# Output projection of the attention block as three half-precision products in place of one 32-bit product

## The reference, cut to what matters

```
q, k, v = x @ wq.T, x @ wk.T, x @ wv.T          # 16 heads of 64; rotary embedding on q and k
probs = softmax(causal(q @ k.T * scale))
out = probs @ v                                 # (4, 1024, 1024)
out = einsum('btd,od->bto', out, wo)            # output projection, (4, 1024, 128)
x = x + layernorm(out); then the feed-forward part
```

## Time and profile before

| what | value |
|---|---|
| time, median of 3 runs | 1192.29 us (1190.64 to 1192.48) |
| the profiled execution's own time | 1189.41 us |
| its span, first to last instruction | 1187.5 us |
| busy share PE, PEld | 93%, 67% |
| busy share DVE, ACT, POOL | 81%, 81%, 80% |
| granted TensorE clock, mean share of full speed | 0.978 |
| slots 0 to 15 of the attention loop | 62.4 to 941 us |
| feed-forward part | 947 to 1187.5 us |

### The profile page before, as it was taken

One profiled execution on the slowest core, in us unless ns is written; L12 is line 12 of the kernel. 1 busy time (PEld: TensorE's weight loads), 2 busy tenths in 40 slices (PEclk: granted clock), 3 DMA queues, 4 the chain that ended last, 5 costly groups with the idle time before them and its releaser, 6 DMA issues. The chain is left out here.

```text
span 1187.5 us, 36496 instructions
## 1 busy us (share of the span) xinstructions
PE 1110.2 (93%) x14311; PEld 800.0 (67%) x14311; DVE 959.2 (81%) x2195; ACT 956.4 (81%) x2205; POOL 951.1 (80%) x1064
## 2 busy tenths in 40 slices
PE   4689999999999999999999999999998788999996
PEld 1256777777777777777777777777776555666663
DVE  7789787978879797979788797979895359767977
ACT  7767989889797979798897979798887767756574
POOL 3569899999999999999999999999784567434663
PEclk9689999999999999999999999999998999999999
DMA  6761525252533425152515345252611000000011
GB/s 194 167 151 38 144 49 132 73 126 57 143 82 99 106 75 145 39 142 73 134 48 143 79 103 121 61 145 54 163 32 39 15 23 2 1 1 1 2 37 36
DMA packets 50475, 97.24 MB, mean 82 GB/s; under 512 B 8512, under 2 KB 25152, under 8 KB 46272
## 3 DMA queue, kind: packets, MB, share of 16 engines
q1 hardware_dynamic: 50304, 94.92, 31.6%
HBM read 58.47 MB, written 34.60 MB: 78 GB/s over the span
## 5 line engine op out<-in xcount | busy, mean ns | idle before, releaser
L916 POOL TENSOR_TENSOR Plo<-P,Phi 128x512 f16<-128x512 f32 (+3 forms) x634 | 531.6, 866 | 68.1 <-ACT P L566 66.4
L563 ACT ACTIVATE Phi<-psS 128x512 f16<-128x512 f32 (+3 forms) x768 | 394.6, 514 | 125.3 <-PE psS L413 74.1
L566 ACT ACTIVATE P<-psS 128x512 f32<-128x512 f32 (+3 forms) x634 | 313.8, 496 | 0.0
L435 PE MATMUL psO<-V,Plo 128*128 128x65 f16 x2304 | 289.2, 194 | 0.0
L431 PE MATMUL psO<-V,Phi 128*128 128x65 f16 x2304 | 288.6, 193 | 0.6 <-POOL Plo L916 0.6
L433 PE MATMUL psO<-V,Phi 128*128 128x64 f16 x2304 | 287.5, 192 | 0.0
L402 PE MATMUL psS<-Q,K 128*128 128x512 f16 (+3 forms) x768 | 252.8, 329 | 17.6 <-DVE Plo L742 13.0
L431 PEld LDWEIGHTS psO<-V,Phi 128*128 128x128 f16 x2304 | 216.1, 98 | 42.5 <-POOL Plo L916 1.4
L791 DVE TENSOR_REDUCE pmax<-psX 128x1 f32<-128x512 f32 x384 | 242.1, 681 | 0.2
L433 PEld LDWEIGHTS psO<-V,Phi 128*128 128x128 f16 x2304 | 214.9, 97 | 31.2 <-issue 1.1
L435 PEld LDWEIGHTS psO<-V,Plo 128*128 128x128 f16 x2304 | 214.4, 97 | 0.0
(11 more groups left out here) (215 smaller groups left out, 2500.7 us busy)
## 6 DMA issues: line engine op xcount, KB each, us to landing
k_way<-HL SPq DMA_DIRECT2D x64, 256.0 KB, 3.9
K<-k_way SPq DMA_DIRECT2D x32, 512.0 KB, 8.4
q_way<-HL SPq DMA_DIRECT2D x60, 256.0 KB, 3.7
Q<-q_way SPq DMA_DIRECT2D x15, 1024.0 KB, 11.8
K<-k_way SPq DMA_DIRECT2D x32, 256.0 KB, 4.3
Q<-q_way SPq DMA_DIRECT2D x30, 256.0 KB, 5.3
out<-y SPq DMA_DIRECT2D x8, 256.0 KB, 2.2
y<-in_x SPq DMA_DIRECT2D x3, 512.0 KB, 10.4
```

The costliest lines, as they stand in the source:

```text
L435: mm = nc.tensor.matmul(O, M.Plo[:, U % NP_, k * P:(k + 1) * P], V[:, HD:2 * HD + 1], start=False, stop=j == t, skip_group_check=True)
L563: nc.scalar.activation(M.Phi[:, U % NP_, 0:w], X, ACT.Exp, scale=SCALE)
L566: nc.scalar.activation(full, X, ACT.Exp, scale=SCALE).then_inc(S.exp_done, 1)
L916: nc.gpsimd.tensor_tensor(M.Plo[:, U % NP_, 0:w], M.P32[:, U % NP_, 0:w], M.Phi[:, U % NP_, 0:w], ALU.subtract).then_inc(S.lo_pool, 1)
```

## The change

The product is made of 16-bit halves. The transposed output is split by ScalarE (upper half, the same copy as before with a 16-bit output) and by VectorE (lower half: the bank minus the upper half), as is done for V. VectorE now gives the bank back, and `wo` waits for that. The weights are split once: their 32-bit form comes by the same DMA into the second half of `M.OT`, which is free then; ScalarE copies the upper halves at slot 0, step 20, and GpSimd forms the lower ones at step 26. For each chunk TensorE adds three products: upper by upper, upper weights by lower outputs, and lower weights by upper outputs (the product of the two lower halves is left out).

```diff
+WO_HALVES = ((0, 20), (0, 26))
 TR1_STEPS, WO_STEPS, TR0_STEPS = (10, 16), (17, 18), (33, 46)
...
+    ot32 = M.OT[:].rearrange("p w a n -> p (w a n)").bitcast(F32)
+    wo32 = ot32[:, TT * D:2 * TT * D].rearrange("p (k d) -> p k d", d=D)
...
                     if s == 1 and half == 0:
-                        pe.wait_ge(S.wo_in, 16)
+                        pe.wait_ge(S.wo_lo, 1)
                     taken(pe, (s - 1, "tr", 0, half))
                     taken(pe, (s, "tr", 1, half))
                     for k in range(4):
                         for c in range(CH):
                             t = 4 * half + k
-                            mm = nc.tensor.matmul(X[:, k * P:(k + 1) * P], M.OT[:, c, t * P:(t + 1) * P],
-                                                  M.wo[:, CH * og + c, :], start=c == 0, stop=c == CH - 1)
+                            for q, (wi, xi) in enumerate([(0, 0), (0, 1), (1, 0)]):
+                                mm = nc.tensor.matmul(X[:, k * P:(k + 1) * P], M.OT[:, xi, c, t * P:(t + 1) * P],
+                                                      M.wo[:, wi, CH * og + c, :], start=c == 0 and q == 0,
+                                                      stop=c == CH - 1 and q == 2)
...
-                    nc.scalar.copy(M.OT[:, a[0], a[1] * BANK:(a[1] + 1) * BANK], X).then_inc(free(item), 1)
+                    nc.scalar.copy(M.OT[:, 0, a[0], a[1] * BANK:(a[1] + 1) * BANK], X).then_inc(S.turn_hi, 1)
...
+                if (s, u) == WO_HALVES[0]:
+                    act.wait_ge(S.wo_in, 16)
+                    nc.scalar.copy(M.wo[:, 0], wo32).then_inc(S.wo_hi, 1)
...
+                elif kind == "tr":
+                    dve.wait_ge(S.turn_hi, turn[item] + 1)
+                    if turn[item] == 0:
+                        dve.wait_ge(S.wo_lo, 1)
+                    cols = slice(a[1] * BANK, (a[1] + 1) * BANK)
+                    nc.vector.tensor_tensor(M.OT[:, 1, a[0], cols], X, M.OT[:, 0, a[0], cols],
+                                            ALU.subtract).then_inc(free(item), 1)
...
+                if (s, u) == WO_HALVES[1]:
+                    pool.wait_ge(S.wo_hi, 1)
+                    nc.gpsimd.tensor_tensor(M.wo[:, 1], wo32, M.wo[:, 0], ALU.subtract).then_inc(S.wo_lo, 1)
...
-            sp.dma_start(M.wo[:], I["wo"]).then_inc(S.wo_in, 16)
+            sp.dma_start(wo32, I["wo"]).then_inc(S.wo_in, 16)
...
-        M.wo = sb(stack, "wo", [P, HEADS * HD // P, D], F32)
+        M.wo = sb(stack, "wo", [P, 2, HEADS * HD // P, D], F16)
...
-        M.OT = sb(stack, "OT", [P, CH, T], F32)
+        M.OT = sb(stack, "OT", [P, 2, CH, T], F16)
```

More of the change, by code:

```diff
@@ L313, in attention_block @@
     weights = (M.wkq[:, 0], M.wkq[:, 1], M.wv)
+    ot32 = M.OT[:].rearrange("p w a n -> p (w a n)").bitcast(F32)
+    wo32 = ot32[:, TT * D:2 * TT * D].rearrange("p (k d) -> p k d", d=D)
+    turn = {}
+    for key in steps:
+        for item in at.get(key, []):
+            if item[1] == "tr":
+                turn[item] = len(turn)
     w32 = M.P32[:].rearrange("p a n -> p (a n)").rearrange("p (k n) -> p k n", k=3)
@@ L627, in junk @@
             def junk(n):
-                to = M.On if n < 3 * TT else M.OT
                 k = (n - TT) % (2 * TT)
-                return to[:].rearrange("p a n -> p (a n)")[:, k * D:(k + 1) * D]
+                if n < 3 * TT:
+                    return M.On[:].rearrange("p a n -> p (a n)")[:, k * D:(k + 1) * D]
+                return ot32[:, k * D:(k + 1) * D]
             def x_sums(b):
@@ L1961, in build @@
         S.wo_in = sem("wo_in")
+        S.wo_hi = sem("wo_hi")
+        S.wo_lo = sem("wo_lo")
+        S.turn_hi = sem("turn_hi")
         S.w_lo_pool = sem("w_lo_pool")
```

## The result

| kernel | median, us | runs | against the kernel before |
|---|---|---|---|
| before | 1191.11 | 5 | 1 |
| changed | 1199.42 (1198.03 to 1201.86) | 5 | 1.0076, 95% interval 1.0057 to 1.0094 |

The change makes the kernel slower by 0.8%. The profiled execution of the changed kernel took 1201.86 us, the highest of the five, and that of before 1189.41 us, so their difference (12.5 us) is larger than that of the medians (8.3 us).

The account below looks back on a forecast made before the run. It took a chain through GpSimd, ScalarE, VectorE and TensorE as the bound, over GpSimd at the projection. 14 x 0.71 = +9.9, weights +1.0, end -0.5 make +10.4 us; forecast 1201 us, range 1184 to 1213.

Parts of the forecast that it names:

- the saving: Projection on TensorE: 1.04 us a slot spared, 16.6 us in all at most; taken as bringing 0.
- the subtractions at steps 10 and 16: VectorE's added work on chunk 1's transposes: each taken at 0; bounds at step 10 were 0 and 0.60 us.
- the term for step 33: VectorE waits 0.95 us for ScalarE's copy, subtracts ahead of out_scale, delays TensorE: 0.7 us a slot, bounds 0 and 1.55.
- The price of an item: Each projection item on TensorE takes 1.34 us as half-precision products, in place of 1.87 and 1.86 us.
- The new wait: Step 17: the first projection item waits for step 16's subtraction and starts 0.48 us later, so its gain is gone.
- The closed chain: Around a slot: GpSimd up to step 27, ScalarE to step 36, VectorE for one operation, TensorE and ScalarE for the rest.
- GpSimd's unbroken stretch: GpSimd runs 461.31 to 494.69 without a wait; the second item's 0.52 us lie beside it and don't shorten it.
- Step 46 at 0: VectorE's subtraction there is covered by VectorE's own free time: 0, bounds 0 and 0.6 us.
- rival 3: VectorE becomes the bound in steps 8 to 40: 1.7 us a slot lost, 1216 us; chance 0.13.
- The last projection: After the last slot: two items of 1.34 us and a subtraction end it at 945.18, 0.5 us gained.
- The weights' split: Slot 0: one ScalarE copy and one GpSimd operation, taken at 1.0 us, bounds 0 and 2.1.
- The first, TensorE holds the slot: Rival: each slot gets 1.04 us shorter, 1175.7 us in full, 1184 for half; chance 0.29.

Follow-up runs that it names:

- Products only: Changed kernel without VectorE's subtractions, upper half standing in for the lower, ScalarE giving the bank back: 1172.58 us, 0.9853 of the kernel before.
- one step later: Changed kernel with VectorE alone taking the subtraction of step 33 one step later, behind out_scale: 1196.02 us, 1.0053 of the kernel before.
- no lower at 33: Changed kernel without the subtraction at step 33, upper half standing in for the lower: 1192.59 us, 1.0023 of the kernel before.
- subtraction only: Kernel before, 32-bit projection kept, plus VectorE's 64 subtractions into a scratch tile that nothing reads: 1208.75 us, 1.016 of the kernel before.
- lower at 46 alone: Changed kernel with only the subtraction at step 46 kept, upper half standing in elsewhere: 1176.13 us, 0.9877 of the kernel before.

## Why the prediction was right, and where its steps failed

**Direction and size were right**: 1201 forecast, 1199.4 measured; 0.71 us a slot forecast, 0.73 measured in a slot without a DMA wait and 0.97 as the mean. But this is luck in part. Three terms of a slot, each taken at 0, were not 0: the saving, -1.04 us, and the subtractions at steps 10 and 16, +0.60 each. Together they make +0.16, about what the term for step 33 was too high.

**The price of an item** was right: 1.34 us, 1.05 us spared per slot.

**"The new wait" of the first item was wrong.** I read the waits ahead of `wo` as if item 0 needed the subtraction of step 16. `taken(pe, (s, "tr", 1, half))` asks for that of its own half, step 10, which is long done. There is no wait, and both items give back their 0.52 us.

**The closed chain, and "lie beside GpSimd's unbroken stretch", were wrong.** I took a stretch of 33 us without a wait as the sign of the engine that sets the pace, and closed the chain with ScalarE's wait for the last Plo of it. Products only showed neither to hold: the wait behind GpSimd's stretch shrank by 0.84 us, and ScalarE's wait at step 28 was for TensorE's scores, which had come within 0.01 us of that Plo. The sign I gave too little weight was TensorE's own: its idle times sum to 0.40 us in slot 7 of the kernel before. The saving was taken at 0; in products only it is 1.06 us in a slot without a DMA wait, and in the changed kernel 1.02 - 0.64 = 0.38 is left of it. The subtraction at step 16 takes the rest.

**Step 10 and step 16, each taken at 0,** cost 0.60 us each: the upper bound that I gave for step 10. The cover named for them, GpSimd's stretch, wasn't one.

**Step 33 was right in its mechanism and somewhat too high.** The wait was 0.90 us (0.95 forecast), and TensorE's delay in steps 33 to 37 0.81 us (0.71). I had the chain without slack until it closes, but 0.26 us come back in steps 37 to 41, so that 0.54 of the 0.71 is left. The wait for V was swallowed on VectorE and not on TensorE, as forecast; it went from 1.07 us to none, where I had some 0.6 left. That the order ahead of `out_scale` is the cause was shown in the trace of "one step later".

**Step 46 at 0 was right.** So was the sign against rival 3: GpSimd's wait for VectorE at step 28 is 1.03 us in the changed kernel and didn't grow.

**The ends.** The last projection was to gain 0.5 us. From the last scores to the last sum it took 10.37 us and 9.22 before, 1.15 more. That is the clock: "no lower at 33" does the same there at the full clock and takes 8.87, a gain of 0.35. The weights' split was taken at 1.0 us; slot 0 took 67.1 us in both kernels by the same events, and its steps 19 to 33, where the split stands, 15.95 in both, so it costs nothing. Slot 14, where I had no loss, got shorter by 2.4 us (50.5 to 48.1): 1.06 in steps 17 to 19, TensorE's saving, and 1.6 in steps 41 to 48, where the kernel before had waited 1.42 us for the DMA of the row maxima and the changed one didn't.

**The sum again** with the measured terms: -1.02 + 0.60 + 0.60 + 0.54 + 0 = 0.72 us a slot, 0.73 in slot 7. By the rule of the Trainium skill (Perfetto Trace Analysis, section Identifying the Most-Contended Engine) that I weighed, to judge TensorE's headroom by the busy share of its weight loads, TensorE had a quarter of its time free (76%). In products only 1.04 us spared on TensorE made slot 7 shorter by 1.06 us, so the trace disagrees with the rule, and the measurement decides.

**The rivals.** The first, TensorE holds the slot, is true of the kernel before and would have decided had nothing been added to VectorE. The third, VectorE becomes the bound, is true of its price and not of its reason: the subtractions at steps 10, 16 and 33 cost 1.74 us a slot together, against which 1.02 us are saved; the rival had counted 1.7 us and no saving. But VectorE relieved of 0.60 us at step 8 brought nothing; what costs is where a subtraction stands between a copy and a bank.

## What to carry to other kernels

An engine that runs long without a wait isn't therefore the one that sets the pace: look also for an engine that has next to no idle time in the whole period, here TensorE with 0.40 us of 53.91, and at the wait behind the long stretch, here 1.02 us. A wait that two engines end within 0.01 us of each other says nothing of which of them it was for; the program's own wait conditions do. Where work moves from one engine to another inside a tight pipeline, measure each half alone: here -17 us and +19 us, and together +8. An operation that waits for another engine should stand behind those of its engine that wait for nothing; moving a subtraction one step back was worth 0.54 us a slot in the trace with no change in the work. And before a difference of some tenths of a us per slot is read as the change's, look at how much single slots differ within one trace: here up to 1.5 us, from a DMA.

## What the runs showed of the hardware

**The clock at the end.** Every trace has a short stretch of half clock within some 15 us of the last projection: ahead of it, on it or behind it. In the kernel before it ends before the last scores, in the changed one and in subtraction only it meets the last projection (granted 0.50 and 0.55). The idle time of TensorE ahead of that projection doesn't tell which: it was 0.33 us before, 0.65 in the changed kernel and 1.06 in subtraction only, but "no lower at 33" has 1.05 at the full clock and "lower at 46 alone" 0.33 at half clock. Timelines of TensorE, the first kernel and then the second:

```profile
945.87 2.84 PE L543 MATMUL psX<-wo,OT 128*128 128x128 f16 x48 [1.05 <-DVE OT L798]
```

```profile
928.81 4.29 PE L543 MATMUL psX<-wo,OT 128*128 128x128 f16 x48 [0.33 <-ACT OT L621]
```

The same 48 half-precision products took 2.84 us at the full clock and 4.29 where the granted clock was 0.50 for the first 3.1 of them. The 32 records of 32-bit products took 3.81 us at the full clock and 6.68 in subtraction only. What decides where the stretch falls is open.

**The DMA at a slot's start.** In each trace TensorE waits in two to five slots for the DMA of the row maxima, up to 1.4 us, and otherwise not. What decides in which slots is open as well.
